# First attention of an early-fusion transformer: values of two steps in a row every second step, and PSUM banks moved from plain scores to turned scores

## What is computed

```python
def _L0_attn_ref(x, ln_g, ln_b, Wq, bq, Wk, bk, Wv, bv):
    ...
    q = (xn @ Wq + bq).reshape(B, T, H, D // H)
    k = (xn @ Wk + bk).reshape(B, T, H, D // H)
    v = (xn @ Wv + bv).reshape(B, T, H, D // H)
    attn = jnp.einsum('bnhd,bmhd->bnmh', q, k) * scale
    w = jax.nn.softmax(attn, axis=2)
    y = jnp.einsum('bnmh,bmhd->bnhd', w, v).reshape(B, T, D)
...
h = h + _L0_attn_ref(_layernorm(h, axis=-1), ...)
```

## Time and profile before

| | us |
|---|---|
| median of three executions | 2065.36 (2063.44 to 2066.84) |
| the profiled execution, its own time | 2068.74 |
| its span in the trace | 2067.0 |
| TensorE matmuls busy | 1769.8 (86%) |
| DVE busy | 1084.6 (52%) |
| ACT busy | 753.2 (36%) |

### The profile page before, as it was taken

One profiled execution on the slowest core, in us unless ns is written; L12 is line 12 of the kernel. 1 busy time (PEld: TensorE's weight loads), 2 busy tenths in 40 slices (PEclk: granted clock), 3 DMA queues, 4 the chain that ended last, 5 costly groups with the idle time before them and its releaser, 6 DMA issues. The chain is left out here.

```text
span 2067.0 us, 33185 instructions
## 1 busy us (share of the span) xinstructions
PE 1769.8 (86%) x10034; PEld 1222.8 (59%) x10034; DVE 1084.6 (52%) x3556; ACT 753.2 (36%) x1859; POOL 552.2 (27%) x728
## 2 busy tenths in 40 slices
PE   4599999996997989978784999968899898885998
PEld 3244444444664767746553999846666666663766
DVE  6477676764226766654544222266666666751111
ACT  1144444451321234422221111166656666632121
POOL 0111010003002122221113333333544445543334
PEclk9899999998997989989996999979999999997999
DMA  5744353518700000040113666360100000003351
GB/s 188 139 92 99 77 107 66 99 22 243 312 0 0 1 1 1 1 163 21 27 27 89 229 215 211 109 176 8 28 22 20 21 21 21 21 21 87 118 171 48
DMA packets 90239, 171.74 MB, mean 83 GB/s; under 512 B 26086, under 2 KB 73417, under 8 KB 82558
## 3 DMA queue, kind: packets, MB, share of 16 engines
q1 hardware_dynamic: 67849, 149.47, 25.8%
q0 software_dynamic: 20480, 18.35, 3.3%
q10 hardware_dynamic: 1764, 2.23, 0.6%
HBM read 111.75 MB, written 61.87 MB: 84 GB/s over the span
## 5 line engine op out<-in xcount | busy, mean ns | idle before, releaser
L2556 POOL TENSOR_SCALAR l_P<-l_P,l_ri 111x111 f32<-111x111 f32 (+1 forms) x256 | 178.1, 713 | 178.4 <-DVE l_ri L2729 178.1
L790 ACT ACTIVATE PT<-psT 111x666 f32<-111x666 f32 x192 | 139.4, 726 | 165.6 <-PE psT L888 165.3
L2814 ACT ACTIVATE l_P<-l_S,l_nm 111x111 f32<-111x111 f32 (+2 forms) x384 | 179.3, 471 | 24.8 <-DVE l_nm L2722 24.5
L687 DVE TENSOR_REDUCE mx<-psS 111x2 f32<-111x666 f32 x192 | 159.6, 847 | 30.1 <-PE psS L873 30.1
L899 PE MATMUL psO<-PT,vS 111*32 111x333 f32 x768 | 147.4, 463 | 0.1
L2972 PE MATMUL l_psP<-ident,l_P 111*111 111x111 f32 x768 | 102.6, 270 | 32.5 <-DVE l_PT L2738 26.7
L2972 PEld LDWEIGHTS l_psP<-ident,l_P 111*111 111x111 f32 x768 | 90.1, 179 | 62.8 <-issue 34.5
L2722 DVE CUSTOM_DVE_ANT_0 l_S<-l_psA,l_am 111x111 f32<-111x111 f32 (+1 forms) x256 | 79.1, 330 | 70.5 <-PE l_psA L2958 64.9
L2338 PEld LDWEIGHTS t_psH<-t_xT,expert_w 128*128 128x128 f32 x896 | 105.8, 194 | 1.3
L2338 PE MATMUL t_psH<-t_xT,expert_w 128*128 128x128 f32 x896 | 105.8, 277 | 0.0
L638 POOL TENSOR_TENSOR low<-raw,high 128x333 f32<-128x333 f32 x32 | 28.6, 894 | 276.9 <-DVE high L699 276.9
(11 more groups left out here) (473 smaller groups left out, 3701.7 us busy)
## 6 DMA issues: line engine op xcount, KB each, us to landing
expert_w<-in_moe_dram SPq DMA_DIRECT2D x36, 1024.0 KB, 5.2
xs_scratch<-zeros SPq DMA_DIRECT2D x27, 896.0 KB, 24.3
c_w<-in_moe_dram SPq DMA_DIRECT2D x16, 1024.0 KB, 7.7
qs<-halves_scratch SPq DMA_DIRECT2D x128, 83.5 KB, 3.2
ks<-halves_scratch SPq DMA_DIRECT2D x112, 83.5 KB, 3.8
halves_scratch<-high SPq DMA_DIRECT2D x32, 167.0 KB, 2.5
halves_scratch<-low SPq DMA_DIRECT2D x32, 167.0 KB, 3.2
h_scratch<-h SPq DMA_DIRECT2D x16, 288.0 KB, 2.4
```

What stands on the lines that cost most here:

```text
L687: v.tensor_reduce(mx[J % 2][:, t, c:c + 65:64], psS[s % 2][0:TT, :, 0:T], AX.X, ALU.max, negate=True).then_inc(max_done, 1)
L790: s_.activation(PT[jp % 2][:, :, a, :], psT[0:TT, :, 0:T], ACT.Exp).then_inc(exp_done, 1)
L2556: r = g.tensor_scalar(Pt, Pt, ri[:, c % 2, 2 * t + half:2 * t + half + 1], None, ALU.mult)
L2814: s_.activation(P[c % 4][:, half, at(t):at(t + 1)], Sm[:, half, at(t):at(t + 1)], ACT.Exp, bias=nm[:, c % 2, i:i + 1], scale=-1.0, accum_o ...
```

## The change

Three things change. The banks: `psS` becomes one pair and `psT` two, used in turn. So plain scores of step s wait for the maximum of step s - 1, and turned scores for the exponentials of step s - 2. The values: odd steps do those of s - 3 and s - 2, one after the other, and even steps none. The table AT: most pieces behind the first move to other steps, so that eleven even steps and five odd ones have one; before, five even steps and eleven odd ones had one. What is computed stays the same, and no instruction is added or taken away except waits.

```diff
-        psS = [pb2(f"psS{i}") for i in range(2)]
-        psT = pb2("psT")
+        psS = pb2("psS")
+        psT = [pb2(f"psT{i}") for i in range(2)]
...
-        AT = [(1, "x", 0), (2, "x", 1), (3, "qk", 0), (4, "qk", 1), (5, "most", 1), (6, "ot", 3), (7, "qk", 2),
-              (8, "qk", 3), (9, "ot", 0), (11, "most", 2), (12, "v", 0), (13, "v", 1), (15, "ot", 1), (17, "most", 3),
-              (21, "ot", 2), (23, "most", 0)]
+        AT = [(1, "x", 0), (2, "x", 1), (4, "qk", 0), (5, "most", 1), (6, "ot", 3), (7, "qk", 1), (8, "qk", 2),
+              (9, "ot", 0), (10, "qk", 3), (11, "most", 2), (12, "v", 0), (14, "v", 1), (16, "most", 3), (18, "ot", 1),
+              (20, "ot", 2), (22, "most", 0)]
...
-                v.tensor_reduce(mx[J % 2][:, t, c:c + 65:64], psS[s % 2][0:TT, :, 0:T], AX.X, ALU.max,
+                v.tensor_reduce(mx[J % 2][:, t, c:c + 65:64], psS[0:TT, :, 0:T], AX.X, ALU.max,
...
-                s_.activation(PT[jp % 2][:, :, a, :], psT[0:TT, :, 0:T], ACT.Exp).then_inc(exp_done, 1)
+                s_.activation(PT[jp % 2][:, :, a, :], psT[s % 2][0:TT, :, 0:T], ACT.Exp).then_inc(exp_done, 1)
...
-                if some(NS * b + s - 1):
-                    pe.wait_ge(max_done, NS * b + s - 1)
+                if some(NS * b + s):
+                    pe.wait_ge(max_done, NS * b + s)
...
-                if some(NS * b + s):
-                    pe.wait_ge(exp_done, NS * b + s)
+                if some(NS * b + s - 1):
+                    pe.wait_ge(exp_done, NS * b + s - 1)
...
-                    if s >= 2:
-                        values(b, p, s - 2)
-                    elif not first:
-                        values(b - 1, 1 - p, NS + s - 2)
+                    if s % 2 == 1:
+                        for n in (s - 3, s - 2):
+                            if n >= 0:
+                                values(b, p, n)
+                            elif not first:
+                                values(b - 1, 1 - p, NS + n)
```

More of the change, by code:

```diff
@@ L513, in attention16 @@
         sc_tmp = sb("sc_tmp", [TT, 3, NT])
-        psS = [pb2(f"psS{i}") for i in range(2)]
-        psT = pb2("psT")
+        psS = pb2("psS")
+        psT = [pb2(f"psT{i}") for i in range(2)]
         psO, psM = pb("psO"), pb("psM")
-        first_bank = [psM, psO, psS[0][:, 0, :], psS[0][:, 1, :], psS[1][:, 0, :], psS[1][:, 1, :], psT[:, 0, :],
-                      psT[:, 1, :]]
+        first_bank = [psM, psO, psS[:, 0, :], psS[:, 1, :], psT[1][:, 0, :], psT[1][:, 1, :], psT[0][:, 0, :],
+                      psT[0][:, 1, :]]
         (consts, xn_ready, high_ready, low_ready, s_done, mx_ready, max_done, st_done, exp_done, pv_done, o_out,
@@ L866, in scores @@
                         pe.wait_ge(stack_in[n], 128 * (b + 1))
-                if isinstance(b, int) and b == 0 and s < 2:
-                    pe.wait_ge(piece_out, 4 + 2 * s)
-                if some(NS * b + s - 1):
-                    pe.wait_ge(max_done, NS * b + s - 1)
+                if isinstance(b, int) and b == 0 and s == 0:
+                    pe.wait_ge(piece_out, 4)
+                if some(NS * b + s):
+                    pe.wait_ge(max_done, NS * b + s)
                 for half in range(2):
                     ph = slice(64 * half, 64 * half + 64)
-                    r = mm(psS[s % 2][0:TT, half, 0:TE], qs[p][ph, jp, qt(t)], ks[p][ph, jp, :], start=True, stop=True)
+                    r = mm(psS[0:TT, half, 0:TE], qs[p][ph, jp, qt(t)], ks[p][ph, jp, :], start=True, stop=True)
                 r.then_inc(s_done, 1)
@@ L880, in scores_less_most @@
                     pe.wait_ge(piece_out, most_place(b, jp // 2, first, last) + 1)
-                if some(NS * b + s):
-                    pe.wait_ge(exp_done, NS * b + s)
+                if some(NS * b + s - 1):
+                    pe.wait_ge(exp_done, NS * b + s - 1)
                 for half in range(2):
                     ph = slice(64 * half, 64 * half + 64)
-                    mm(psT[0:TT, half, 0:TE], ks[p][ph, jp, qt(a)], qs[p][ph, jp, :], start=True, stop=False)
+                    mm(psT[s % 2][0:TT, half, 0:TE], ks[p][ph, jp, qt(a)], qs[p][ph, jp, :], start=True, stop=False)
                 for half in range(2):
                     ph = slice(64 * half, 64 * half + 64)
-                    r = mm(psT[0:TT, half, 0:TE], spread[ph, jp % 2, :], mT[jp // 2 % 2][ph, :], start=False, stop=True)
+                    r = mm(psT[s % 2][0:TT, half, 0:TE], spread[ph, jp % 2, :], mT[jp // 2 % 2][ph, :], start=False, stop=True)
                 r.then_inc(st_done, 1)
```

## The result

The changed kernel takes 2098.9 us (median of four executions, 2095.31 to 2100.95), the kernel before 2066.1 beside it (2063.44 to 2068.71). The ratio is 1.0159, with a 95% interval from 1.0141 to 1.0178: slower by 32.8 us, where 44.5 were forecast. The profiled execution took 2098.81 us and its span is 2097.1, 30.1 more than before.

A forecast was written before the change was run, and what follows sets the result against it. TensorE was taken as the bound, without room in a batch of the first attention. Opening 6, batch 0 6, six middle batches 28 and last batch 4.5 summed to +44.5 us: about 2110 us, range 2090 to 2128.

The forecast's parts named there:

- The opening's +6: Nine plain scores in a row at the low clock, 1.59 us each with one pair: 12.7 us instead of 6.5.
- the sum gave +4.7: Middle batch: stalls of 7.5 us against 2.8 saved, 45.1 to 49.8 us by slots; six batches, +28.
- -2.6 (0.9 + 1.2 + 0.5): Savings per batch: values directly behind values 0.9 us, couples across column groups 1.2, waits for the one psT 0.5.
- +5.7 (1.44 + 2.68 + 1.56): Waits for the maximum per batch: behind transposing pieces 1.44 us, behind pieces' DVE work 2.68, step 1 behind xn 1.56.
- +1.65 (1.85 - 0.2): Per batch: closer pieces waiting for psM add 1.85 us; step 0, without piece or values, saves 0.2.
- the second term of what the change takes away: Four couples per batch in different column groups: second step's first pair runs with first step's second, 0.30 each, 1.2 us.
- the range that the prediction left open there: Values behind values: 0.61 instead of 0.68 us taken; the whole 0.21 us per change of matmul kind would give 2.7 us.
- +6 was forecast, bounds 4 and 9: Batch 0: as other batches, plus six blocks of entry statistics, each 2.0 us of DVE between maxima, only partly covered.
- colder opening (+2): One of four additions to the forecast's high end of 2128 us: 2 us more from a colder opening.
- Rival 2: Stalls of 1 to 1.6 us drop TensorE's clock, about 3.9 us each, 27 us more: 2137 us; 6 in 100.
- Rivals 1, 3 and 4: Maximum hidden, 2047 us, 5 in 100; next batch's scores wait for q/k, 2125 us, 5 in 100; couples don't overlap, 2115.
- Rival 4: Couples don't overlap across column groups: +0.6 to 0.7 us per batch, 2115 us; counted inside the main case, no own chance.

The follow-up runs named there:

- e2_banks_alone: The kernel before with only the new banks (one pair psS, two pairs psT), its own values and table: 2114.35 us, ratio 1.023.
- e5_half_max: The changed kernel with DVE's maximum taken over only half the columns of each head's scores: 2069.49 us, ratio 1.0008.
- e1_old_banks: The changed kernel with the banks of before (two pairs psS, one pair psT), couples and new table kept: 2061.63 us, ratio 0.9976.
- e4_same_columns: The changed kernel with the values of every head pair in the same two column groups: 2106.02 us, ratio 1.0206.
- e9_statistics_early: The changed kernel with four of the six blocks of entry statistics moved ahead of the first maximum: 2098.18 us, ratio 1.0149.
- e3_table_alone: The kernel before with only the new table AT: 2065.91 us, ratio 1.0008.
- e6_four_couples_old_table: The kernel before, its banks and table, with only four couples of values per batch, in different column groups: 2063.58 us, ratio 0.9979.

## Why the prediction was right, and where its sum was off

**The mechanism is shown.** One pair `psS` serialises TensorE and DVE (`e2_banks_alone`, +48 us), its price hangs on the length of the maximum (`e5_half_max`, -31), and it is gone with two pairs (`e1_old_banks`, about -38). The opening's +6 is exact: 15.19 - 9.13 = 6.06; 1.57 per load was measured, 1.59 forecast.

**A middle batch: +2.3 where the sum gave +4.7.** The slots of batch 4, added up by kind from one weight load to the next of another line, before and after:

| slots, us | before | after | difference | forecast |
|---|---|---|---|---|
| values | 17.05 | 12.75 | -4.30 | -2.6 (0.9 + 1.2 + 0.5) |
| turned scores, with the wait for the maximum | 6.00 | 11.56 | +5.56 | +5.7 (1.44 + 2.68 + 1.56) |
| plain scores, with the wait for `psM` | 9.44 | 10.43 | +0.99 | +1.65 (1.85 - 0.2) |
| pieces | 12.89 | 12.89 | 0 | 0 |
| period | 45.38 | 47.64 | +2.26 | +4.7 |

The term most mis-sized is the second term of what the change takes away, "0.30 each, 1.2 us" for the couples in different column groups. That a second step's first pair runs with the first step's second pair was the wrong picture: both steps run together, all eight matmuls in 0.77 us, so a couple holds TensorE for 0.70, not 0.99. Four of them are 4 x 0.29 = 1.2 us more. The Trainium skill, page TensorEngine Tiling (Array Packing), section Key Properties, says that different tiles can load weights and run matmuls in parallel; the 0.77 us agree with it. The prediction weighed that section's rule on draining and not this one beside it.

Two smaller sizes. The couples of one head pair save 2 x 0.684 - 1.245 = 0.12 each instead of 0.07 (8 x 0.05 = 0.4). That settles the range that the prediction left open there: a removed change of kind is worth neither 0.07 nor the whole 0.21 us. And plain scores that had to wait hold TensorE for 0.335 instead of 0.39, since their matmuls start at once (load and matmul both at 302.18): ten slots of this length, and the four that wait for `psM` are counted so too, 14 x 0.055 = 0.8 us. For the same reason the hand-over is 1.36 and not 1.43. Together 1.2 + 0.4 + 0.8 = 2.4, which is the gap.

The stalls agree with the forecast, 5.56 and 5.7, also term by term: about 1.4 in the even steps with a transposing piece (1.44 forecast), 2.9 behind DVE's part of the pieces (2.68) and 1.3 behind the three `xn` (1.56). So do the waits for `psM` with 2.0 and 1.85 (slots of 1.05 ahead of `ot` 3, 1.07 ahead of `v` 0, 0.71 ahead of q/k 3 and 0.54 ahead of `x` 1, less 0.335 each). But in part this is luck: shorter couples make more stalls, by `e4_same_columns` about half of what they save. With couples of 0.99 the stalls would have come to about 5.0 us (5.56 less half of 1.2), so the forecast had them some 0.7 too large. By the same reckoning the mis-sized couples shorten the batch itself by only about 0.6 us; the rest of the gap is the two smaller sizes and the stalls.

**Batch 0: +7.6 where +6 was forecast, bounds 4 and 9.** The number is within its bounds, and partly by luck. The forecast gave the excess over a middle batch to the blocks of statistics and, but for a "colder opening (+2)" at its high end, nothing to the clock. But batch 0 has some 11 us more of low clock than before. What a microsecond of it costs can be estimated twice: 3.9 us for the 10 us behind a back edge, which is the prediction's own figure, and 55.63 - 53.85 = 1.78 us for the 3.6 us that batch 3 has more than batch 5. At 0.4 to 0.5 us each the 11 us make 4.4 to 5.5 us, and with the 2.3 of a clean batch that is 6.7 to 7.8, nearly all of the 7.6. So little is left for stalls of the statistics at full clock; they count as far as they bring the clock down (`e9_statistics_early` takes 4.0 us off the batch in its trace, with three falls gone and one new). How much of the low clock is due to the change stays open: `e1_old_banks` and `e3_table_alone` have the opening of before, and yet a mean clock of 0.90 and 0.91 over batch 0, 9 to 10 us of low clock against 4, and take 49.61 and 50.32 us against 48.91.

**Rival 2, the clock falls, is true in four places.** It was forecast as 3.9 us at each of seven batches. Instead, the undisturbed batches keep 1.00 with a stall of 1.3 us at step 1, and only where stalls pile up, at 114, 148 and 155 us and in the last batch at 475, does it fall. Batch 1 begins at the low clock and takes 50.21 instead of about 47.7 us. The reading of the stretch 94 to 143 us before as evidence against it was fair for the middle batches and not for batch 0.

**Back edges.** Taken as +4.7 each, like any batch: batch 3 costs 2.3 more, as a clean batch does, and batch 5 only 0.3. In batch 5 the low clock lasts about 6.5 us where it lasted 10 before, which at the price above is 1.4 to 1.8 of the missing 2.0 us. Why it was shorter was not tested. **The last batch** costs 3.7, forecast 4.5, and has a fall of the clock that the forecast did not count.

**Rivals 1, 3 and 4.** The maximum isn't hidden; `e5_half_max` shows how far it would have to shrink. Plain scores of the next batch do not wait for q and k: in the waits of after, 84 to 520 us, none is for a DMA. Rival 4, that couples don't overlap, was made true by `e4_same_columns` and costs 7 to 10 us by times whose intervals just overlap, 1.1 us in a middle batch of the trace, where the prediction had 5 and 0.6 to 0.7. Two pairs of heads in other column groups save more than it thought.

**The signs named before.** Waits for the maximum 67.9 us (55 to 75 said), on 91 of 192 loads (over a third). First turned scores at 99.11 (about 100). Couples 1.25 and 0.70 (1.29 and 0.99). Middle batches 47.7 (50). The waits of `psT` for ACT's `PT` are 21.0 us and not below 5. None of them is over 0.54 us, and the row at 308.36 shows what 33 of the 43 are: turned scores behind a couple of values, whose load has 0.54 us of idle time, as at 305.12, where it is put down to issue. The slot is 0.70 us with it. (The other ten stand behind pieces, at 0.24 to 0.35 us.) The sign was a bad one: the same idle time stands behind values whoever is named beside it.

**The whole.** 6.1 (opening) + 7.6 (batch 0) + 14.2 (batches 1 to 6) + 3.7 (last) = 31.6, and the attention's scores start 0.7 us earlier: 30.9, against 30.1 in the span. Forecast were 6 + 6 + 28 + 4.5. The miss of about 12 us is the six batches 1 to 6 (-14), with +1.6 in batch 0 against it; two of the six are not clean, for batch 1 costs 2.4 us more than a clean one by its low clock, and batch 5 some 2 us less.

## What to carry to other kernels

Count for every pair of PSUM banks the time from the first write to the release, with all other work that the releasing engine has in between, and compare it with what TensorE has to do until it wants the pair again; the double buffer belongs where the most is missing. The bare chains are alike here: 1.36 us for plain scores, and 0.25 + 1.13 = 1.38 for turned ones (`e6_four_couples_old_table`), both against about 1.1 of work in an even step with a short piece. What differs is the work beside them: about 1.4 of the 5.56 us of stalls in batch 4 belong to the bare chain, and 4.2 to DVE's part of the pieces and to `xn`. That this makes plain scores the ones to keep two pairs for is read from the slots; the runs show that the kernel with two pairs of them is 38 us faster at the same couples and table.

Two small matmul groups that lie in different column groups are worth putting side by side: the second added 0.01 us here. Two in the same group save only 0.12 us. And stalls close together can cost clock too, as at the end of batch 0.

## What the runs showed of the hardware that was not expected

- Four pairs of fp32 matmuls (111 rows, 32 columns, 333 long) in four different column groups ran in 0.77 us, and the next kind of matmul could load 0.70 us after the first. The same eight in two column groups took 1.31 and 1.25.
- Plain scores that had waited for their banks held TensorE for 0.335 us, those that followed other work directly for 0.39.
- Granted clock: 1.00 in 310 to 357 us, with TensorE busy for 43.21 of 47 us and single stalls of up to 1.3 us; 0.50 behind stretches in which it was busy for 2.41 and 2.09 of 4 us; and 0.77 in one stretch of `e9_statistics_early` where it was busy for 3.01 of 4. In the changed kernel from 204 to 208 us it was busy for 2.79 of 4, and the clock stayed at 1.00 there and in the next 4 us.
- Behind a back edge of the loop the low clock lasted about 10 us in one batch of the changed kernel and about 6.5 in another, and the two batches took 55.63 and 53.85 us.
